# Fused attention block, 8 rows a group: row constant and shift by plain tensor additions, x transposes moved on the TensorE queue

## The chip, the cores and the metric

One core of a Trainium2 chip runs the whole kernel. The metric is the device time of the launch in microseconds; lower is better. Before the change the median of 3 runs is 5887.01 us (5886.72 to 5887.08).

## What is computed

The input `x` has shape (64, 128, 128, 64) in float32: 8192 independent rows of 128 tokens with 64 channels. With all names cut down, the reference is

```python
xn = (x - mean) * rsqrt(var + 0.001) * gamma + beta
q, k, v = xn @ Wq + bq, xn @ Wk + bk, xn @ Wv + bv
scores = einsum('bhid,bhjd->bhij', q, k) * 64 ** -0.5
out = softmax(scores, -1) @ v
return xn + out @ Wo + bo
```

## The kernel before, in words

**Folding.** The normalization and the weights are folded once at the start. Per row of tokens the kernel then needs `g = w_g^T x + g_bias`, scores `g^T x`, softmax, `u = x^T P^T` and `o = u^T w_o`. The output is `y = attn + x_scaled_rows`, where `attn` is `o` times the inverted sum of the softmax and `x_scaled_rows` is the residual with all output biases.

**Shift of the softmax.** The exponential takes a negative shift as its bias. The row constant is the dot product of `x` with a weight row (`row_const`, a reduction over 64 channels of the second half of `x_weighted`) plus a scalar `const_bias`. `top` is that plus the row maximum of the scores (`row_max`); `neg_top` is that minus `top`. Each of these is 128x8 (8 rows of a group).

**Tiling.** A group is 8 rows (`GROUP`), 1024 groups in all. All engines work through the same software pipeline: `pipeline` calls `step(r, t, peeled)` for each t; inside the loop body 8 steps are unrolled, and every engine's queue is the order written by hand in its own `step`. Tiles have 2, 4 or 8 buffers, with rings of semaphores counting their uses.

**Order on each engine in step t** (the number is the group):

- GpSimd (POOL): `x_weighted`(t+2), line 231, 128x1024, after `const_found`(t); `x_scaled_rows`(t+2), line 236; `y`(t-3), line 245, after `attn`(t-3). All three are tensor_tensor instructions with both inputs in SBUF.
- VectorE (DVE): reciprocal `inv_sum`(t-3), line 365; `attn`(t-3), line 370; `row_max`(t), line 376, after the scores; copy `uT`(t-2), line 385; `top`(t), line 392; `neg_top`(t), line 395; `row_const`(t+1), line 401, after `x_weighted`(t+1); copy `xT`(t+2), line 409, after the x transposes.
- TensorE (PE): scores(t), line 456; `u`(t-2) into `ux_ps`, line 467, after `xT`(t+1) is copied out of that bank; first half of the probability transposes (t-1), line 443; `g`(t+1), line 483; second half of them (t-1), line 443 too; x transposes (t+2) into `ux_ps`, line 498, after `uT`(t-2) is copied out; `o`(t-2), line 508.
- ScalarE (ACT): copy of the first transposed half (t-1), line 264; `g`(t+1), line 271; copy of the second half (t-1), line 277; eight exponentials (t), line 287, after `neg_top`(t).
- SyncE (SP): load of group t+4, store of group t-3.

`attn` reads `o_ps` (PSUM) and `inv_sum` (SBUF); `row_max`, `uT` and `xT` read PSUM alone; the `row_const` reduction reads one SBUF tensor; `top` and `neg_top` read two SBUF tensors and one pointer scalar from SBUF.

Of the kernel before, what the change touches and what calls it, by code (L numbers as in the profile page):

```python
# [11 lines left out]
GROUP = 8  # L12
# [5 lines left out]
def build(nc: bass.Bass, x, gamma, beta, mean, var, wq, bq, wk, bk, wv, bv, wo, bo, out):  # L18
# [10 lines left out]
    with ExitStack() as ctx:  # L29
        def sb(name, shape, dtype=F32):  # L30
            return ctx.enter_context(nc.sbuf_tensor(name, shape, dtype))
# [7 lines left out]
        def sem_ring(name, size=SEMS):  # L39
            return [sem(f"{name}{i}") for i in range(size)]  # L40
# [4 lines left out]
        g = sb("g", [128, 4, PAIRS, W])  # L45
        x_weighted = sb("x_weighted", [128, 2, GROUP, 2, C])
        x_scaled_rows = sb("x_scaled_rows", [128, 8, GROUP, C])
        row_const = sb("row_const", [128, 4, GROUP])
        row_max = sb("row_max", [128, 4, GROUP])
        top = sb("top", [128, 4, GROUP])  # L50
# [49 lines left out]
        max_found = sem_ring("max_found")  # L100
        top_found = sem_ring("top_found")
        neg_top_found = sem_ring("neg_top_found")
        const_found = sem_ring("const_found")
        probs_a_found = sem_ring("probs_a_found")
        probs_b_found = sem_ring("probs_b_found")
# [104 lines left out]
        @block.gpsimd  # L210
        def _(pool):
            nc.gpsimd.memset(ident[:], 0.0).then_inc(pool_const, 1)
            nc.gpsimd.memset(w_g[:], 0.0).then_inc(pool_const, 1)
            nc.gpsimd.memset(w_o[:], 0.0).then_inc(pool_const, 1)
            pool.wait_ge(pool_const, POOL_CONSTS)
            nc.gpsimd.affine_select(out=ident[:], in_=ident[:], compare_op=ALU.not_equal, fill=1.0, base=0,
                                    pattern=[[-1, 128]], channel_multiplier=1).then_inc(pool_const, 1)

            weights_b = row_weights[:, None, :, :].broadcast_to([128, GROUP, 2, C])
            bias_b = out_bias[:, None, :].broadcast_to([128, GROUP, C])  # L220
            pool.wait_ge(dve_setup, DVE_READY)

            def step(r, t, peeled):
                n = t + 2
                if exists(r, n, peeled):
                    s = parts(n)
                    pool.wait_ge(x_loaded[n % 8], load_uses(r, n))
                    if exists(r, n - 2, peeled):
                        pool.wait_ge(const_found[parts(n - 2)], uses(r, n - 2))
                        pool.wait_ge(x_scaled[parts(n - 2)], uses(r, n - 2))  # L230
                    nc.gpsimd.tensor_tensor(x_weighted[:, n % 2], x_in[:, n % 8, :, None, :].broadcast_to([128, GROUP, 2, C]),  # L231
                                            weights_b, ALU.mult).then_inc(x_weighed[s], 1)
                    pool.wait_ge(x_weighed[s], uses(r, n))
                    if exists(r, n - 8, peeled):
                        pool.wait_ge(y_found[s], uses(r, n - 8))
                    nc.gpsimd.tensor_tensor(x_scaled_rows[:, n % 8], x_weighted[:, n % 2, :, 0, :], bias_b,  # L236
                                            ALU.add).then_inc(x_scaled[s], 1)
                n = t - 3
                if exists(r, n, peeled):
                    s = parts(n)  # L240
                    pool.wait_ge(attn_kept[s], uses(r, n))
                    pool.wait_ge(x_scaled[s], uses(r, n))
                    if exists(r, n - 4, peeled):
                        pool.wait_ge(y_stored[s], dma_uses(r, n - 4))
                    nc.gpsimd.tensor_tensor(y[:, s], attn[:, s], x_scaled_rows[:, n % 8], ALU.add).then_inc(y_found[s], 1)  # L245

            pipeline(pool, step, dma=True)
# [49 lines left out]
        def _(dve):  # L297
# [62 lines left out]
            def step(r, t, peeled):  # L360
                n = t - 3
                if exists(r, n, peeled):
                    s = parts(n)
                    dve.wait_ge(probs_b_found[s], uses(r, n))
                    nc.vector.reciprocal(inv_sum[:, s, :], prob_sum[:, s, :]).then_inc(sum_inverted[s], 1)  # L365
                    dve.wait_ge(sum_inverted[s], uses(r, n))
                    dve.wait_ge(o_made[s], uses(r, n))
                    if exists(r, n - 4, peeled):
                        dve.wait_ge(y_found[s], uses(r, n - 4))  # L369
                    nc.vector.tensor_tensor(attn[:, s], o_rows, inv_sum[:, s, :, None].broadcast_to([128, GROUP, C]),  # L370
                                            ALU.mult).then_inc(attn_kept[s], 1)
                n = t
                if exists(r, n, peeled):
                    s = parts(n)
                    dve.wait_ge(scores_made[s], uses(r, n))
                    nc.vector.tensor_reduce(row_max[:, s, :].rearrange("p (k h) -> p h k", h=2),  # L376
                                            score_ps[n % 2][:].rearrange("p h (k w) -> p h k w", k=PAIRS),
                                            AX_X, ALU.max).then_inc(max_found[s], 1)
                n = t - 2
                if exists(r, n, peeled):  # L380
                    s = parts(n)
                    dve.wait_ge(u_made[s], uses(r, n))
                    if exists(r, n - 2, peeled):
                        dve.wait_ge(o_made[parts(n - 2)], uses(r, n - 2))
                    nc.vector.tensor_copy(uT[:, n % 2], ux_ps[:].rearrange("p (k w) -> p k w", k=PAIRS)) \  # L385
                        .then_inc(u_kept[s], 1)
                n = t
                if exists(r, n, peeled):
                    s = parts(n)
                    dve.wait_ge(max_found[s], uses(r, n))  # L390
                    dve.wait_ge(const_found[s], uses(r, n))
                    nc.vector.scalar_tensor_tensor(top[:, s, :], row_const[:, s, :], const_bias[:, 0:1], row_max[:, s, :],  # L392
                                                   ALU.add, ALU.add).then_inc(top_found[s], 1)
                    dve.wait_ge(top_found[s], uses(r, n))
                    nc.vector.scalar_tensor_tensor(neg_top[:, s, :], row_const[:, s, :], const_bias[:, 0:1], top[:, s, :],  # L395
                                                   ALU.add, ALU.subtract).then_inc(neg_top_found[s], 1)
                n = t + 1
                if exists(r, n, peeled):
                    s = parts(n)
                    dve.wait_ge(x_weighed[s], uses(r, n))  # L400
                    nc.vector.tensor_reduce(row_const[:, s, :], x_weighted[:, n % 2, :, 1, :],  # L401
                                            AX_X, ALU.add).then_inc(const_found[s], 1)
                n = t + 2
                if exists(r, n, peeled):
                    s = parts(n)
                    dve.wait_ge(xT_made[s], uses(r, n))
                    if exists(r, n - 4, peeled):
                        dve.wait_ge(scores_made[s], uses(r, n - 4))
                    nc.vector.tensor_copy(xT[:, s], ux_ps[:].rearrange("p (k w) -> p k w", k=PAIRS)) \  # L409
                        .then_inc(xT_kept[s], 1)  # L410

            pipeline(dve, step)

        @block.tensor
        def _(pe):
# [30 lines left out]
            def step(r, t, peeled):  # L446
# [31 lines left out]
                if exists(r, n, peeled):  # L478
                    s = parts(n)
                    pe.wait_ge(xT_kept[s], uses(r, n))  # L480
                    if exists(r, n - 1, peeled):
                        pe.wait_ge(g_kept[parts(n - 1)], uses(r, n - 1))
                    nc.tensor.matmul(g_ps[:], w_g_all, xT[:, s].rearrange("p k w -> p (k w)"),  # L483
                                     start=True, stop=True).then_inc(g_made[s], 1)
                n = t - 1
                if exists(r, n, peeled):
                    s = parts(n)
                    pe.wait_ge(probs_b_found[s], uses(r, n))
                    pe.wait_ge(probsT_a_kept[s], uses(r, n))
                    transposed_probs(n, HALF).then_inc(probsT_b_made[s], 1)  # L490
                n = t + 2
                if exists(r, n, peeled):
                    s = parts(n)
                    pe.wait_ge(x_loaded[n % 8], load_uses(r, n))
                    if exists(r, n - 4, peeled):
                        pe.wait_ge(u_kept[parts(n - 4)], uses(r, n - 4))
                    for k in range(PAIRS):
                        last = nc.tensor.transpose(ux_ps[:, k * W:(k + 1) * W],  # L498
                                                   x_in[:, n % 8, 2 * k:2 * k + 2, :].rearrange("p s c -> p (s c)"), ident[:])
                    last.then_inc(xT_made[s], 1)  # L500
                n = t - 2
                if exists(r, n, peeled):
                    s = parts(n)
# [29 lines left out]
```

## Time and profile before

| what | value |
|---|---|
| median of 3 runs | 5887.01 us |
| the profiled execution | 5891.6 us |
| its span (first to last instruction) | 5889.8 us |
| PE busy | 5650.5 us (96%) |
| DVE busy | 5769.4 us (98%) |
| ACT busy | 4783.0 us (81%) |
| POOL busy | 4992.3 us (85%) |
| granted TensorE clock, mean | 0.999 |
| HBM traffic over the span | 91 GB/s |

The profiled execution is 4.6 us above the median. Busy time of an engine counts from an instruction's start to its end as recorded, and it includes time in which an instruction that has started stands still. A steady step of the pipeline works on one group on each engine, so the span is near 1024 times the length of a step plus the filling and draining. In a timeline, the time between the starts of neighbouring instructions on one engine says more than their durations, since neighbouring instructions can overlap by some tens of nanoseconds.

### The profile page before, as it was taken

Reading aid. Unit: us, or ns where it says so; the run is one execution under the profiler, and the core shown is the slowest. Engines: PE = TensorE matmul, PEld = TensorE weight load, DVE = VectorE, ACT = ScalarE, POOL = GpSimd, SP = SyncE. Lnnn points to the kernel's source line nnn. Section 1 sums busy time; section 2 is a strip of 40 time slices with the busy share of each in tenths; the row PEclk is TensorE's granted clock in tenths of the full one; section 3 lists DMA queues with packets and bytes.
Section 4 is the critical chain, followed back from the end, with each engine's and each line's share of the span. In section 5 each row is a group of like instructions: output and inputs, shape, how many; then the busy total and the mean of one; then the engine's idle time right before and its main releaser. Section 6 shows DMA issues by size and latency. Waiting matters only on the chain.

```text
span 5889.8 us, 169868 instructions
## 1 busy us (share of the span) xinstructions
PE 5650.5 (96%) x55320; PEld 4441.6 (75%) x55320; DVE 5769.4 (98%) x8226; ACT 4783.0 (81%) x19460; POOL 4992.3 (85%) x3080
## 2 busy tenths in 40 slices
PE   7999999999999999999999999999999999999999
PEld 6777777777777777777777777777777777777777
DVE  8999999999999999999999999999999999999999
ACT  6888888888888888888888888888888888888887
POOL 7888888888888888888888888888888888888887
PEclk9999999999999999999999999999999999999999
DMA  3444444444444444444444444444444444444443
GB/s 76 91 93 93 92 91 91 93 93 91 91 92 93 93 91 91 93 93 92 91 91 93 93 91 91 92 93 93 91 91 92 93 92 91 91 93 93 91 91 85
DMA packets 2131546, 537.56 MB, mean 91 GB/s; under 512 B 2131520, under 2 KB 2131520, under 8 KB 2131520
## 3 DMA queue, kind: packets, MB, share of 16 engines
q1 hardware_dynamic: 2131520, 537.23, 41.6%
q8 instruction: 14, 0.23, 0.0%
q14 instruction: 12, 0.10, 0.0%
HBM read 268.67 MB, written 268.44 MB: 91 GB/s over the span
## 4 chain that ended last, share of the span: by engine, by line
PE 68%; DVE 23%; issue 8%; DVEq 1%; POOL 0%; SPq 0%; ACT 0%; DMA 0%; POOLq 0%
PE probsT_ps L443 17%; PE ux_ps L467 17%; PE o_ps L508 14%; PE g_ps L483 13%; DVE xT L409 11%; DVE row_const L401 8%; PE ux_ps L498 7%; DVE top L392 2%; DVE uT L385 1%; DVE row_max L376 1%; DVEq L369 1%; DVEq L156 0%; DVE inv_sum L365 0%; PE score_ps L456 0%; POOL y L245 0%
## 5 line engine op out<-in xcount | busy, mean ns | idle before, releaser
L287 ACT ACTIVATE probs<-score_ps,neg_top 128x128 f32<-128x128 f32 x8192 | 2874.9, 376 | 686.1 <-DVE neg_top L395 686.1
L231 POOL TENSOR_TENSOR x_weighted<-x_in,row_weights 128x1024 f32<-128x1024 f32 x1024 | 2427.1, 2370 | 789.1 <-issue 675.9
L287 ACT ACTIVATION_READ_ACCUMULATOR probs<-score_ps,neg_top 128x1 f32 x8192 | 1765.5, 216 | 0.0
L443 PEld LDWEIGHTS probsT_ps<-ident,probs 128*128 128x128 f32 x8192 | 859.0, 140 | 915.0 <-issue 727.4
L236 POOL TENSOR_TENSOR x_scaled_rows<-x_weighted,out_bias 128x512 f32<-128x512 f32 x1024 | 1307.4, 1277 | 90.8 <-POOL x_weighted L231 20.2
L443 PE MATMUL probsT_ps<-ident,probs 128*128 128x128 f32 x8192 | 1315.5, 283 | 5.9 <-ACT probs L287 3.7
L467 PE MATMUL ux_ps<-probsT,x_in 128*64 128x128 f32 x16384 | 1120.8, 278 | 203.1 <-DVE xT L409 176.7
L245 POOL TENSOR_TENSOR y<-attn,x_scaled_rows 128x512 f32<-128x512 f32 x1024 | 1301.6, 1271 | 13.8 <-DVE attn L370 13.8
L395 DVE SCALAR_TENSOR_TENSOR neg_top<-row_const,const_bias,top 128x8 f32<-128x8 f32 x1024 | 1217.1, 1189 | 36.3
L376 DVE TENSOR_REDUCE row_max<-score_ps 128x8 f32<-128x1024 f32 x1024 | 1243.4, 1214 | 2.2 <-PE score_ps L456 2.0
L456 PE MATMUL score_ps<-xT,g 64*128 64x128 f32 x16384 | 1190.0, 285 | 0.3 <-ACT g L271 0.3
L467 PEld LDWEIGHTS ux_ps<-probsT,x_in 128*64 128x64 f32 x16384 | 895.9, 136 | 376.2 <-issue 300.9
L456 PEld LDWEIGHTS score_ps<-xT,g 64*128 64x128 f32 x16384 | 993.9, 187 | 124.2 <-ACT g L271 1.1
L508 PE MATMUL o_ps<-w_o,uT 128*128 128x128 f32 x8192 | 1082.1, 275 | 0.8 <-DVE uT L385 0.8
L483 PE MATMUL g_ps<-xT,w_g 128*128 128x512 f32 x2048 | 1050.3, 595 | 0.9 <-DVE xT L409 0.9
L508 PEld LDWEIGHTS o_ps<-w_o,uT 128*128 128x128 f32 x8192 | 995.3, 192 | 1.0 <-DVE uT L385 1.0
L271 ACT ACTIVATE g<-g_ps,g_bias 128x512 f32<-128x512 f32 x1024 | 703.8, 687 | 290.4 <-PE g_ps L483 290.3
L392 DVE SCALAR_TENSOR_TENSOR top<-row_const,const_bias,row_max 128x8 f32<-128x8 f32 x1024 | 816.6, 798 | 0.1
L370 DVE TENSOR_TENSOR attn<-o_ps,inv_sum 128x512 f32<-128x512 f32 x1024 | 707.9, 691 | 53.0 <-issue 5.7
L264 ACT ACTIVATE probsT<-probsT_ps 128x512 f32<-128x512 f32 x1024 | 611.5, 597 | 107.3 <-PE probsT_ps L443 3.0
L385 DVE COPY uT<-ux_ps 128x512 f32<-128x512 f32 x1024 | 696.8, 680 | 0.6 <-PE ux_ps L467 0.6
L409 DVE COPY xT<-ux_ps 128x512 f32<-128x512 f32 x1024 | 690.8, 675 | 3.8 <-PE ux_ps L498 3.8
(66 smaller groups left out, 2908.1 us busy)
## 6 DMA issues: line engine op xcount, KB each, us to landing
x_in<-in_x SPq DMA_DIRECT2D x1024, 256.0 KB, 3.2
out<-y SPq DMA_DIRECT2D x1024, 256.0 KB, 2.8
norm_row<-in_L_conv_gamma SPq DMA_DIRECT2D x1, 32.0 KB, 3.7
norm_row<-in_L_conv_beta SPq DMA_DIRECT2D x1, 32.0 KB, 3.7
norm_row<-in_L_conv_moving_mean SPq DMA_DIRECT2D x1, 32.0 KB, 4.2
norm_row<-in_L_conv_moving_var SPq DMA_DIRECT2D x1, 32.0 KB, 4.3
norm_row<-in_L_conv_bo SPq DMA_DIRECT2D x1, 32.0 KB, 4.5
w_raw<-in_L_conv_Wq SPq DMA_DIRECT2D x1, 16.0 KB, 1.9
```

Of the source, the lines that this page charges most:

```text
L231: nc.gpsimd.tensor_tensor(x_weighted[:, n % 2], x_in[:, n % 8, :, None, :].broadcast_to([128, GROUP, 2, C]), weights_b, ALU.mult).then_inc ...
L236: nc.gpsimd.tensor_tensor(x_scaled_rows[:, n % 8], x_weighted[:, n % 2, :, 0, :], bias_b, ALU.add).then_inc(x_scaled[s], 1)
L245: nc.gpsimd.tensor_tensor(y[:, s], attn[:, s], x_scaled_rows[:, n % 8], ALU.add).then_inc(y_found[s], 1)
L287: last = nc.scalar.activation(probs[:, n % 2, q, :], score_ps[n % 2][:, q % 2, q // 2 * W:(q // 2 + 1) * W], ACT.Exp, bias=neg_top[:, s, q ...
L376: nc.vector.tensor_reduce(row_max[:, s, :].rearrange("p (k h) -> p h k", h=2), score_ps[n % 2][:].rearrange("p h (k w) -> p h k w", k=PAIR ...
L395: nc.vector.scalar_tensor_tensor(neg_top[:, s, :], row_const[:, s, :], const_bias[:, 0:1], top[:, s, :], ALU.add, ALU.subtract).then_inc(n ...
L409: nc.vector.tensor_copy(xT[:, s], ux_ps[:].rearrange("p (k w) -> p k w", k=PAIRS)) \
L443: last = nc.tensor.transpose(probsT_ps[:, (q - first) * W:(q - first + 1) * W], probs[:, n % 2, q, :], ident[:])
L456: last = nc.tensor.matmul(score_ps[n % 2][:, h, k * W:(k + 1) * W], g[half, s, k, :], xT[half, s, k, :], start=True, stop=True)
L467: last = nc.tensor.matmul(ux_ps[h * C:(h + 1) * C, k * W:(k + 1) * W], x_in[:, n % 8, 2 * k + h, :], probsT[:, n % 2, 2 * k + h, :], start ...
L483: nc.tensor.matmul(g_ps[:], w_g_all, xT[:, s].rearrange("p k w -> p (k w)"), start=True, stop=True).then_inc(g_made[s], 1)
L508: last = nc.tensor.matmul(o_ps[:, k * 2 * C:(k + 1) * 2 * C], uT[:, n % 2, k, :], w_o_all, start=True, stop=True)
```

## The change

`row_const` is now made in two instructions: the reduction writes `row_part`, and a tensor_tensor addition of `const_bias`, broadcast over the 8 rows, writes `row_const` at the end of the DVE step, behind the `xT` copy. `top` and `neg_top` become tensor_tensor instructions without a pointer scalar. POOL's wait for the free `x_weighted` buffer is now on `part_found`. On PE the x transposes (t+2) come ahead of the second half of the probability transposes (t-1).

```diff
+        row_part = sb("row_part", [128, 4, GROUP])
...
+        part_found = sem_ring("part_found")
...
                     if exists(r, n - 2, peeled):
-                        pool.wait_ge(const_found[parts(n - 2)], uses(r, n - 2))
+                        pool.wait_ge(part_found[parts(n - 2)], uses(r, n - 2))
                         pool.wait_ge(x_scaled[parts(n - 2)], uses(r, n - 2))
...
                     dve.wait_ge(max_found[s], uses(r, n))
                     dve.wait_ge(const_found[s], uses(r, n))
-                    nc.vector.scalar_tensor_tensor(top[:, s, :], row_const[:, s, :], const_bias[:, 0:1], row_max[:, s, :],
-                                                   ALU.add, ALU.add).then_inc(top_found[s], 1)
+                    nc.vector.tensor_tensor(top[:, s, :], row_const[:, s, :], row_max[:, s, :],
+                                            ALU.add).then_inc(top_found[s], 1)
                     dve.wait_ge(top_found[s], uses(r, n))
-                    nc.vector.scalar_tensor_tensor(neg_top[:, s, :], row_const[:, s, :], const_bias[:, 0:1], top[:, s, :],
-                                                   ALU.add, ALU.subtract).then_inc(neg_top_found[s], 1)
+                    nc.vector.tensor_tensor(neg_top[:, s, :], row_const[:, s, :], top[:, s, :],
+                                            ALU.subtract).then_inc(neg_top_found[s], 1)
                 n = t + 1
                 if exists(r, n, peeled):
                     s = parts(n)
                     dve.wait_ge(x_weighed[s], uses(r, n))
-                    nc.vector.tensor_reduce(row_const[:, s, :], x_weighted[:, n % 2, :, 1, :],
-                                            AX_X, ALU.add).then_inc(const_found[s], 1)
+                    nc.vector.tensor_reduce(row_part[:, s, :], x_weighted[:, n % 2, :, 1, :],
+                                            AX_X, ALU.add).then_inc(part_found[s], 1)
                 n = t + 2
...
                     nc.vector.tensor_copy(xT[:, s], ux_ps[:].rearrange("p (k w) -> p k w", k=PAIRS)) \
                         .then_inc(xT_kept[s], 1)
+                n = t + 1
+                if exists(r, n, peeled):
+                    s = parts(n)
+                    dve.wait_ge(part_found[s], uses(r, n))
+                    nc.vector.tensor_tensor(row_const[:, s, :], row_part[:, s, :], const_bias[:, 0:1].broadcast_to([128, GROUP]),
+                                            ALU.add).then_inc(const_found[s], 1)
...
                     nc.tensor.matmul(g_ps[:], w_g_all, xT[:, s].rearrange("p k w -> p (k w)"),
                                      start=True, stop=True).then_inc(g_made[s], 1)
-                n = t - 1
-                if exists(r, n, peeled):
-                    s = parts(n)
-                    pe.wait_ge(probs_b_found[s], uses(r, n))
-                    pe.wait_ge(probsT_a_kept[s], uses(r, n))
-                    transposed_probs(n, HALF).then_inc(probsT_b_made[s], 1)
                 n = t + 2
...
                     last.then_inc(xT_made[s], 1)
+                n = t - 1
+                if exists(r, n, peeled):
+                    s = parts(n)
+                    pe.wait_ge(probs_b_found[s], uses(r, n))
+                    pe.wait_ge(probsT_a_kept[s], uses(r, n))
+                    transposed_probs(n, HALF).then_inc(probsT_b_made[s], 1)
```

## Rows read from the trace of the kernel before

**Rows 1.** The page: span, and busy time by engine
```profile
span 5889.8 us, 169868 instructions
PE 5650.5 (96%) x55320; PEld 4441.6 (75%) x55320; DVE 5769.4 (98%) x8226; ACT 4783.0 (81%) x19460; POOL 4992.3 (85%) x3080
```

**Rows 2.** Timeline of DVE, one steady step: start us, us, instruction, [idle before]
```profile
5860.85 0.67 DVE L401 TENSOR_REDUCE row_const<-x_weighted 128x8 f32<-128x512 f32 x1
5861.44 0.67 DVE L409 COPY xT<-ux_ps 128x512 f32<-128x512 f32 x1
5862.04 0.18 DVE L365 RECIPROCAL inv_sum<-prob_sum 128x8 f32<-128x8 f32 x1
5862.26 0.69 DVE L370 TENSOR_TENSOR attn<-o_ps,inv_sum 128x512 f32<-128x512 f32 x1
5862.87 1.21 DVE L376 TENSOR_REDUCE row_max<-score_ps 128x8 f32<-128x1024 f32 x1
5864.00 0.68 DVE L385 COPY uT<-ux_ps 128x512 f32<-128x512 f32 x1
5864.60 0.81 DVE L392 SCALAR_TENSOR_TENSOR top<-row_const,const_bias,row_max 128x8 f32<-128x8 f32 x1
5865.44 1.19 DVE L395 SCALAR_TENSOR_TENSOR neg_top<-row_const,const_bias,top 128x8 f32<-128x8 f32 x1
5866.55 0.67 DVE L401 TENSOR_REDUCE row_const<-x_weighted 128x8 f32<-128x512 f32 x1
```

**Rows 3.** Timelines at the end of the kernel: DVE, then the next POOL instruction
```profile
5870.30 0.22 DVE L392 SCALAR_TENSOR_TENSOR top<-row_const,const_bias,row_max 128x8 f32<-128x8 f32 x1
5870.56 0.23 DVE L395 SCALAR_TENSOR_TENSOR neg_top<-row_const,const_bias,top 128x8 f32<-128x8 f32 x1
5870.70 0.68 DVE L401 TENSOR_REDUCE row_const<-x_weighted 128x8 f32<-128x512 f32 x1
...
5872.81 1.27 POOL L245 TENSOR_TENSOR y<-attn,x_scaled_rows 128x512 f32<-128x512 f32 x1 [2.81 <-DVE attn L370]
```

**Rows 4.** Timeline of POOL in the step of rows 2
```profile
5861.65 2.37 POOL L231 TENSOR_TENSOR x_weighted<-x_in,row_weights 128x1024 f32<-128x1024 f32 x1 [0.75 <-issue]
5864.10 1.29 POOL L236 TENSOR_TENSOR x_scaled_rows<-x_weighted,out_bias 128x512 f32<-128x512 f32 x1
5865.33 1.28 POOL L245 TENSOR_TENSOR y<-attn,x_scaled_rows 128x512 f32<-128x512 f32 x1
```

**Rows 5.** Timelines at the start of the kernel: DVE and POOL
```profile
34.82 2.25 DVE L392 SCALAR_TENSOR_TENSOR top<-row_const,const_bias,row_max 128x8 f32<-128x8 f32 x1
...
34.70 2.35 POOL L231 TENSOR_TENSOR x_weighted<-x_in,row_weights 128x1024 f32<-128x1024 f32 x1
```

**Rows 6.** Instruction groups of DVE: busy us, mean ns | idle before
```profile
L395 DVE SCALAR_TENSOR_TENSOR neg_top<-row_const,const_bias,top 128x8 f32<-128x8 f32 x1024 | 1217.1, 1189 | 36.3
L392 DVE SCALAR_TENSOR_TENSOR top<-row_const,const_bias,row_max 128x8 f32<-128x8 f32 x1024 | 816.6, 798 | 0.1
...
L328 DVE TENSOR_TENSOR b_row<-row_weights,norm_row 128x64 f32<-128x64 f32 x1 | 0.2, 224 | 0.0
...
L322 DVE TENSOR_TENSOR ab_col<-col_tmp,norm_col 64x1 f32<-64x1 f32 x1 | 0.2, 152 | 0.0
```

**Rows 7.** Timeline of PE, one steady step
```profile
5856.56 1.09 PE L467 MATMUL ux_ps<-probsT,x_in 128*64 128x128 f32 x16 [0.21 <-DVE xT L409]
...
5859.02 0.63 PE L443 MATMUL probsT_ps<-ident,probs 128*128 128x128 f32 x4
5859.48 0.60 PE L498 MATMUL ux_ps<-ident,x_in 128*128 128x128 f32 x4
5859.92 1.06 PE L508 MATMUL o_ps<-w_o,uT 128*128 128x128 f32 x8
...
5862.26 1.09 PE L467 MATMUL ux_ps<-probsT,x_in 128*64 128x128 f32 x16 [0.19 <-DVE xT L409]
```

**Rows 8.** Timeline of ACT: the first exponential of the same step
```profile
5860.96 0.37 ACT L287 ACTIVATE probs<-score_ps,neg_top 128x128 f32<-128x128 f32 x1 [0.65 <-DVE neg_top L395]
```

## The prediction

> **What bounds the kernel now.** I read the busy shares first: DVE 98%, PE 96%, ACT 81%, POOL 85% of the span [rows 1]. DVE looks like the bound, and PE close behind. The timeline says what DVE's 98% is made of. One step lasts 5866.55 - 5860.85 = 5.70 us, and two instructions on only 8 elements per partition take 0.84 and 1.11 us of it, counted from start to start [rows 2]. They are not working in that time. At the end of the kernel, while POOL stands idle (its next instruction shows 2.81 us of idle before it, back to 5870.00), the same two take 0.22 and 0.23 us [rows 3].
>
> What they wait for shows in POOL's timeline of the same step [rows 4]. `x_scaled_rows` ends at 5864.10 + 1.29 = 5865.39 and `top` at 5864.60 + 0.81 = 5865.41. `y` ends at 5865.33 + 1.28 = 5866.61 and `neg_top` at 5865.44 + 1.19 = 5866.63. Each ends 0.02 us behind the POOL instruction that was running when it was issued. At the start of the kernel `top` stood for 2.25 us, to 37.07, while POOL's `x_weighted` ran to 37.05 [rows 5]. The means of 798 and 1189 ns over 1024 groups say that this is so all the way [rows 6]. I call this "held": the DVE instruction stands until POOL's is over.
>
> This closes a loop between the two engines. From the start of `row_const`, POOL starts `x_weighted` 0.80 us later, `x_scaled_rows` 2.45 later, `y` 1.23 later, `y` lasts 1.28, `neg_top` is held until its end, and the next `row_const` starts 0.06 before that end: 0.80 + 2.45 + 1.23 + 1.28 - 0.06 = 5.70 us [rows 2, 4]. That is the step. PE fits in: its step is 5.70 with 0.19 us of waiting for `xT`, so 5.51 of its own [rows 7].
>
> **Which instructions are held.** Unheld in the midst of POOL's work run `attn`, a TENSOR_TENSOR with one input in PSUM and one in SBUF (0.69 us, wholly inside `x_weighted`), `inv_sum` with one SBUF input, `row_max` and the copies from PSUM [rows 2, 4]. Three things set `top` and `neg_top` apart: their kind, the pointer scalar, and two tensors that both lie in SBUF. The change takes away the first two and keeps the third. No row shows a plain addition of two SBUF tensors beside a running POOL instruction, so this has to be chosen. A pointer is one value per partition, read once; a second tensor is a stream of its own, and POOL's instructions are streams from SBUF as well. `attn` shows that the plain kind with one such stream goes free, which leaves the second stream as the likeliest cause. I take it: `top` and `neg_top` can still be held, and the new `row_const` addition (`row_part` and the broadcast `const_bias`, both in SBUF) can be held too.
>
> The Trainium skill, page "SBUF — State Buffer", section "Who interferes with whom", says the same: a DVE instruction with two SBUF inputs contends with a GpSimd instruction that reads SBUF, one with at most one such input does not, and the later of the two blocks for the whole of the other. The 2.25 us above agrees with blocking for the whole instruction; by that rule the sum would be the one below.
>
> **The change, part by part.** All times are from the start of the reduction (`row_part`), steps from [rows 2, 4].
>
> *The wait moved to `part_found`*: the same reduction signals, so POOL starts `x_weighted` at 0.80 as before, and ends it at 0.80 + 2.37 = 3.17. Cost nothing.
>
> *The added addition*: the reduction takes 0.59 to the next start, `xT` 0.60, so the addition is issued at 1.19, with `row_part` ready since 0.67. `x_weighted` has been running since 0.80: the addition is held from 1.19 to 3.17 + 0.02 = 3.19. Queued behind it in order are `inv_sum`, `attn`, `row_max`, `uT`, `top`, `neg_top`: everything of the next step. The next starts 0.08 before its end (as the reduction does behind `neg_top` [rows 2]), at 3.11 where it stood at 1.19. DVE loses 1.92 us here.
>
> *The holds that this buys back*: `inv_sum` 3.11, `attn` 3.33 (to 4.02), `row_max` 3.94, `uT` 5.07, `top` issued at 5.67. POOL runs `x_scaled_rows` from 3.25 and `y` from 4.48 (`attn` is ready at 4.02) to 5.76. So `top` is held for at most 0.09 us and `neg_top` not at all, as POOL's next `x_weighted` needs the next reduction. Unheld, the plain additions take: 0.152 us with one element, 0.224 with 64 [rows 6], so about 0.16 with 8. `top` ends at 5.67 + 0.16 = 5.83 (which covers the hold), `neg_top` starts 0.04 later (as in [rows 3]), ends at 6.03, and the reduction starts 0.09 before that [rows 3]: **5.94 us** a step. The bounds: the scalar forms' own times (0.26 and 0.14 from start to start [rows 3]) give 5.67 + 0.40 = 6.07; if the plain additions cost less than 0.16 the end of `y` sets 5.76 + 0.02 + 0.04 + 0.16 - 0.09 = 5.89 at least. I take 5.94, since the nearest rows by kind are the plain additions.
>
> *The x transposes moved ahead*: they need `uT`, which now ends at 5.07 + 0.68 = 5.75. PE then waits for it: the transposes run from about 5.80, the second probability half 0.44 later (6.24), `o` 0.46 after that (6.70), scores and `u`(t-1) start 2.34 - 0.19 = 2.15 after `o` (8.85) [rows 7], end at 9.94, and DVE copies `uT` at 5.07 + 5.94 = 11.01: 1.07 to spare. `xT` needs the transposes at 5.80 + 0.60 = 6.40 and is issued at 5.94 + 0.59 = 6.53: 0.13 to spare. In the old order the transposes would stand behind the second half, which can start 2.46 after `u` [rows 7], at 8.85 - 5.94 + 2.46 = 5.37 or when its copy is through, and would be ready at about 6.43: 0.10 to spare. The move is worth nothing here, at most 0.05 us a step either way. The exponentials cannot start before 5860.96 - 0.65 - 5859.02 = 1.29 us after the second half's start [rows 7, 8], at 7.53 instead of with `neg_top` at 6.03. Who waits for them: ACT is busy 4783.0 / 1024 = 4.67 us a step [rows 1], so 1.27 of a 5.94 us step is free, and the first probability half of the next step is asked for only at 9.94. Nothing.
>
> *Sum*: 5.94 - 5.70 = 0.24 us a step. Over 1024 groups, less a few of filling and draining (some 1015), 244 us. The profiled execution took 5891.6 us; 5891.6 + 244 = 6135.6. It lies 4.6 above the median, so I forecast **6131 us**. The bounds 5.89 and 6.07 give +193 and +376: 6080 to 6263.
>
> **The rivals.**
>
> *Plain additions are not held (faster).* The holds end with the scalar forms. DVE then has 5.70 - 0.84 - 1.11 = 3.75 us of other work and about 0.40 for three additions: 4.15. POOL has 4.96 from the start of `x_weighted` to the end of `y` [rows 4] and no longer waits for DVE's held instruction. PE becomes the bound at 5.51 us: -0.19 a step, -193, **5694 us**. For it: `attn` is of this kind and goes free. Against it: `attn` has one SBUF input.
>
> *Only the two shifts are held, the added one is not (no change).* A broadcast column might not count as a second stream. Then the addition costs 0.08 at 1.19, `top` is issued at 3.75 and held to the end of `x_scaled_rows` at 4.54, `neg_top` to the end of `y`, and the loop of 5.70 stands: **5887 us**. Also the same if the compiler's form were the old one. Nothing in the rows speaks for it but that no broadcast addition is in them.
>
> *All held, and the late `uT` costs more (slower still).* With 0.13 us to spare in front of `xT`, a late `uT` or a wait at the loop's turn shifts PE's transposes behind DVE. Each 0.1 us would add 100 us; with the 6.07 bound and 0.05 of this it would be **6310 us**.
>
> **How the numbers follow.** Held, 5.89 to 6.07 with its own small terms: 0.82. Held with PE's wait on top: 0.04. Not held: 0.09. No change: 0.05. A measurement of this kernel can tell about 0.2%, 12 us, from no change. So slower 0.86, same 0.05, faster 0.09. The range takes the bounds of the held case and some of the third rival: 6075 to 6290; it leaves out the other signs (0.14) and some of the tails.
>
> **What would show it.** If right: the profile of the changed kernel shows the line of the added addition with a mean near 2.0 us, ending 0.02 us behind `x_weighted`; `top` and `neg_top` near 0.16 to 0.2 us; POOL idle about 1.0 us ahead of `x_weighted` (0.80 of it from the reduction); DVE still near 98% busy; PE down to about 93% with its waiting now in front of the x transposes, for `uT`. Wrong at the root: an addition of 0.16 us inside `x_weighted`, DVE near 75% and PE near 99% busy. Wrong in size: `top` held in full by `y`, which would mean that DVE comes round earlier than 5.67, or DVE idle in front of `xT`.

## The result, and the profile after

The changed kernel takes 6140.03 us, median of 4 runs (6139.69 to 6140.2), against 5886.86 us before on the same chip: ratio 1.0431, 95% interval 1.0418 to 1.0443. It is slower by 253 us; 6131 was forecast, in a range of 6075 to 6290. The profiled execution has a span of 6138.2 us.

The page of the changed kernel: its span, its busy times and the costliest group of DVE (busy us, mean ns | idle before):

```profile
span 6138.2 us, 170892 instructions
PE 5661.7 (92%) x55320; PEld 4419.0 (72%) x55320; DVE 6019.2 (98%) x9250; ACT 4793.1 (78%) x19460; POOL 4975.6 (81%) x3080
L417 DVE TENSOR_TENSOR row_const<-row_part,const_bias 128x8 f32<-128x8 f32 x1024 | 1996.6, 1950 | 0.0
```

Two more groups of DVE:

```profile
L397 DVE TENSOR_TENSOR neg_top<-row_const,top 128x8 f32<-128x8 f32 x1024 | 170.7, 167 | 35.4
L394 DVE TENSOR_TENSOR top<-row_const,row_max 128x8 f32<-128x8 f32 x1024 | 161.9, 158 | 0.1
```

The shares of busy time look almost as before [rows 1], and DVE still shows 98%. What fills it is another thing. `top` and `neg_top` fell from 798 and 1189 ns [rows 6] to 158 and 167. The added addition of 8 elements takes 1950 ns on average.

One steady step on DVE (start us, us), as [rows 2]:

```profile
2999.42 0.68 DVE L403 TENSOR_REDUCE row_part<-x_weighted 128x8 f32<-128x512 f32 x1
3000.04 0.69 DVE L411 COPY xT<-ux_ps 128x512 f32<-128x512 f32 x1
3000.65 1.97 DVE L417 TENSOR_TENSOR row_const<-row_part,const_bias 128x8 f32<-128x8 f32 x1
3002.53 0.19 DVE L367 RECIPROCAL inv_sum<-prob_sum 128x8 f32<-128x8 f32 x1
3002.76 0.69 DVE L372 TENSOR_TENSOR attn<-o_ps,inv_sum 128x512 f32<-128x512 f32 x1
3003.37 1.21 DVE L378 TENSOR_REDUCE row_max<-score_ps 128x8 f32<-128x1024 f32 x1
3004.50 0.68 DVE L387 COPY uT<-ux_ps 128x512 f32<-128x512 f32 x1
3005.10 0.15 DVE L394 TENSOR_TENSOR top<-row_const,row_max 128x8 f32<-128x8 f32 x1
3005.29 0.17 DVE L397 TENSOR_TENSOR neg_top<-row_const,top 128x8 f32<-128x8 f32 x1
3005.37 0.68 DVE L403 TENSOR_REDUCE row_part<-x_weighted 128x8 f32<-128x512 f32 x1
```

The same step on POOL, as [rows 4]:

```profile
3000.23 2.36 POOL L233 TENSOR_TENSOR x_weighted<-x_in,row_weights 128x1024 f32<-128x1024 f32 x1 [1.01 <-issue]
3002.67 1.28 POOL L238 TENSOR_TENSOR x_scaled_rows<-x_weighted,out_bias 128x512 f32<-128x512 f32 x1
3003.90 1.27 POOL L247 TENSOR_TENSOR y<-attn,x_scaled_rows 128x512 f32<-128x512 f32 x1
```

The step is 3005.37 - 2999.42 = 5.95 us. The addition is issued 0.42 us after `x_weighted` has started and ends at 3002.62, 0.03 behind it (3002.59). POOL is through with `y` at 3005.17, 0.07 us into `top`, which takes 0.15 us all the same (to 3005.25); `neg_top` meets no POOL instruction. So neither shift is lengthened. Before, the DVE step paid 0.84 and 1.11 us for the shifts. Now it pays 0.19 and 0.08 for them and 1.88 for the addition: 0.20 us more, and 0.05 more for the other instructions together. That is the 5.95 in the place of 5.70.

On PE the waiting has moved in front of the x transposes:

```profile
3003.87 1.02 PE L491 MATMUL g_ps<-xT,w_g 128*128 128x512 f32 x2
3005.33 0.63 PE L500 MATMUL ux_ps<-ident,x_in 128*128 128x128 f32 x4 [0.43 <-DVE uT L387]
3005.79 0.60 PE L451 MATMUL probsT_ps<-ident,probs 128*128 128x128 f32 x4
```

### The profile page after: what moved, and what is told of

The parts are those of the page before. It is cut to its first block, busy times and chain, and to the rows that moved or that the text cites. A ratio compares the mean times of both kernels' runs of the same rounds, so it can differ in the third digit from the quotient of the medians.

```text
span 6138.2 us, 170892 instructions
## 1 busy us (share of the span) xinstructions
PE 5661.7 (92%) x55320; PEld 4419.0 (72%) x55320; DVE 6019.2 (98%) x9250; ACT 4793.1 (78%) x19460; POOL 4975.6 (81%) x3080
## 4 chain that ended last, share of the span: by engine, by line
DVE 38%; issue 31%; PE 29%; DVEq 1%; POOL 0%; SPq 0%; DMA 0%; ACT 0%; POOLq 0%
DVE row_const L417 19%; PE o_ps L516 13%; DVE uT L387 11%; PE ux_ps L500 9%; PE probsT_ps L451 6%; DVE row_max L378 3%; DVE inv_sum L367 2%; DVE row_part L403 1%; DVE attn L372 1%; DVEq L371 1%; DVE xT L411 0%; DVEq L158 0%; DVE top L394 0%; POOL y L247 0%; DVE neg_top L397 0%
## 5 line engine op out<-in xcount | busy, mean ns | idle before, releaser
L417 DVE TENSOR_TENSOR row_const<-row_part,const_bias 128x8 f32<-128x8 f32 x1024 | 1996.6, 1950 | 0.0
L289 ACT ACTIVATION_READ_ACCUMULATOR probs<-score_ps,neg_top 128x1 f32 x8192 | 1856.9, 227 | 0.0
L500 PEld LDWEIGHTS ux_ps<-ident,x_in 128*128 128x128 f32 x4096 | 429.2, 140 | 1261.0 <-issue 1258.8
L247 POOL TENSOR_TENSOR y<-attn,x_scaled_rows 128x512 f32<-128x512 f32 x1024 | 1299.7, 1269 | 15.6 <-DVE attn L372 15.6
L451 PE MATMUL probsT_ps<-ident,probs 128*128 128x128 f32 x8192 | 1286.8, 280 | 4.0 <-ACT probsT L266 2.1
L279 ACT ACTIVATE probsT<-probsT_ps 128x512 f32<-128x512 f32 x1024 | 612.1, 598 | 826.5 <-PE probsT_ps L451 826.5
L500 PE MATMUL ux_ps<-ident,x_in 128*128 128x128 f32 x4096 | 643.3, 280 | 444.6 <-DVE uT L387 442.5
L451 PEld LDWEIGHTS probsT_ps<-ident,probs 128*128 128x128 f32 x8192 | 907.7, 140 | 181.1 <-issue 176.1
L475 PEld LDWEIGHTS ux_ps<-probsT,x_in 128*64 128x64 f32 x16384 | 873.3, 136 | 124.1
L266 ACT ACTIVATE probsT<-probsT_ps 128x512 f32<-128x512 f32 x1024 | 611.5, 597 | 207.1 <-PE probsT_ps L451 207.1
```

The costliest lines, as they stand in the source:

```text
L289: last = nc.scalar.activation(probs[:, n % 2, q, :], score_ps[n % 2][:, q % 2, q // 2 * W:(q // 2 + 1) * W], ACT.Exp, bias=neg_top[:, s, q ...
L417: nc.vector.tensor_tensor(row_const[:, s, :], row_part[:, s, :], const_bias[:, 0:1].broadcast_to([128, GROUP]), ALU.add).then_inc(const_fo ...
L451: last = nc.tensor.transpose(probsT_ps[:, (q - first) * W:(q - first + 1) * W], probs[:, n % 2, q, :], ident[:])
L475: last = nc.tensor.matmul(ux_ps[h * C:(h + 1) * C, k * W:(k + 1) * W], x_in[:, n % 8, 2 * k + h, :], probsT[:, n % 2, 2 * k + h, :], start ...
L500: last = nc.tensor.transpose(ux_ps[:, k * W:(k + 1) * W], x_in[:, n % 8, 2 * k:2 * k + 2, :].rearrange("p s c -> p (s c)"), ident[:])
```

## The experiments

The theory: DVE instructions that need what POOL's instructions use stand until the running POOL instruction ends. The change swaps two short holds for one of nearly the whole of `x_weighted`. Rivals: the scalar form is what gets held; the move on PE costs; one more instruction in the queue costs.

The diffs below are shortened: indices, waits and semaphores are left out, and where only the order changes it is written in words. Each is against the changed kernel, unless the kernel before or another one is named. Each ratio is against the kernel before on the same chip.

### The old order on TensorE

```diff
-    x transposes (t+2), second probability half (t-1)
+    second probability half (t-1), x transposes (t+2)
```

> The changed kernel with the old order on TensorE (second half of the probability transposes ahead of the x transposes). Theory (DVE's queue, with the added addition held by x_weighted, is the loop): the x transposes start when uT is copied in either order, and the second half fits in the idle time in front of them, so the step stays 5.95 us and the time 6140, within 15 us. Rival (the moved transposes carry part of the loss): the time falls by 0.05 to 0.2 us a step, to 5940 to 6090.

Measured: 6143.7 us, ratio 1.0434 (1.0417 to 1.0452) against 1.0431 with the move. PE (in the kernel with the old order) waits at the same place, for the same copy:

```profile
3000.67 0.63 PE L451 MATMUL probsT_ps<-ident,probs 128*128 128x128 f32 x4
3001.61 0.63 PE L506 MATMUL ux_ps<-ident,x_in 128*128 128x128 f32 x4 [0.32 <-DVE uT L387]
```

The move carries none of the loss.

### Only the two shifts as plain additions

```diff
 (the kernel before)
-nc.vector.scalar_tensor_tensor(top, row_const, const_bias, row_max, ALU.add, ALU.add)
+nc.vector.tensor_tensor(top, row_const, row_max, ALU.add)
-nc.vector.scalar_tensor_tensor(neg_top, row_const, const_bias, top, ALU.add, ALU.subtract)
+nc.vector.tensor_tensor(neg_top, row_const, top, ALU.subtract)
```

> The kernel before with top and neg_top as plain additions and nothing added or moved; const_bias is left out of the shift. Theory (a second tensor from SBUF is what gets held, whatever the kind of instruction): both are still held to the ends of x_scaled_rows and y, the loop of 5.70 us stands, 5887 us within 12. Rival (the scalar form is what is held): both take 0.16 us, DVE falls to near 75% busy, PE bounds at 5.51 us, about 5694 us.

Measured: 5886.3 us, ratio 0.9997 (0.9987 to 1.0007). The groups of DVE in this kernel:

```profile
L395 DVE TENSOR_TENSOR neg_top<-row_const,top 128x8 f32<-128x8 f32 x1024 | 1215.6, 1187 | 35.2
L392 DVE TENSOR_TENSOR top<-row_const,row_max 128x8 f32<-128x8 f32 x1024 | 814.9, 796 | 0.1
```

796 and 1187 ns, where the scalar forms had 798 and 1189 [rows 6]. For these two, the scalar form and its pointer make no difference. This settles the choice that the forecast had to make.

### The added instruction with one SBUF input

```diff
-nc.vector.tensor_tensor(row_const, row_part, const_bias.broadcast, ALU.add)
+nc.vector.tensor_reduce(row_const, row_part[:, s, :, None], AX_X, ALU.add)
```

> The changed kernel with the added addition replaced by a reduction over one element, which has one SBUF input and copies row_part; const_bias is left out. Theory: it goes unheld inside x_weighted (about 0.1 us), so top and neg_top come round early again and are held by x_scaled_rows and y: step 5.70, 5887 us within 15. Rival (the extra step in DVE's queue or the move on TensorE costs, not the second input): the time stays above 6000 us.

Measured: 5877.44 us, ratio 0.9981 (0.9971 to 0.9991). The groups of DVE:

```profile
L417 DVE TENSOR_REDUCE row_const<-row_part 128x8 f32<-128x8 f32 x1024 | 147.6, 144 | 0.0
L397 DVE TENSOR_TENSOR neg_top<-row_const,top 128x8 f32<-128x8 f32 x1024 | 1218.2, 1190 | 35.1
L394 DVE TENSOR_TENSOR top<-row_const,row_max 128x8 f32<-128x8 f32 x1024 | 725.9, 709 | 0.1
```

One place in its timeline, DVE and then POOL:

```profile
3007.77 0.14 DVE L417 TENSOR_REDUCE row_const<-row_part 128x8 f32<-128x8 f32 x1
3007.84 0.18 DVE L367 RECIPROCAL inv_sum<-prob_sum 128x8 f32<-128x8 f32 x1
...
3007.38 2.36 POOL L233 TENSOR_TENSOR x_weighted<-x_in,row_weights 128x1024 f32<-128x1024 f32 x1 [0.75 <-issue]
```

At the same place in the queue and with `x_weighted` running, an instruction of the same size is through in 144 ns, and the holds on the shifts are back. `top` takes 0.09 us less than before (709 against 798 ns), near the 0.07 us by which the added instruction puts off the next one: a held instruction absorbs what is put ahead of it.

### The addition ahead of the xT copy

```diff
     reduction -> row_part
+    addition -> row_const
     copy -> xT
-    addition -> row_const
```

> The changed kernel with the addition straight behind the reduction, ahead of the xT copy. Theory (held only if a POOL instruction has already started): it is issued about 0.72 us after the reduction's start, just ahead of x_weighted at 0.80, takes 0.16 us and can push x_weighted back to 0.90 at most; top and neg_top are held again; step 5.70 to 5.80, 5887 to 5990 us. Rival (x_weighted gets in first): held to 3.19 with xT behind it, step 6.54, about 6740 us.

Measured: 5877.4 us, ratio 0.9982 (0.9972 to 0.9991), with all the arithmetic of the changed kernel. That is 10 us below the range that was expected, which took the kernel before for the least. A step of it, DVE and then POOL:

```profile
3003.55 0.67 DVE L403 TENSOR_REDUCE row_part<-x_weighted 128x8 f32<-128x512 f32 x1
3004.26 0.17 DVE L409 TENSOR_TENSOR row_const<-row_part,const_bias 128x8 f32<-128x8 f32 x1
...
3004.36 2.36 POOL L233 TENSOR_TENSOR x_weighted<-x_in,row_weights 128x1024 f32<-128x1024 f32 x1 [0.75 <-issue]
```

The addition starts 0.10 us ahead of `x_weighted` and takes 0.17 us. POOL still starts 0.81 us after the reduction and takes its 2.36 us. So one and the same instruction takes 1.95 us or 0.17 us by its place in DVE's queue: it starts 1.23 us behind the reduction's start or 0.71.

### The addition as tensor_scalar, with a pointer and with an immediate

```diff
-nc.vector.tensor_tensor(row_const, row_part, const_bias.broadcast, ALU.add)
+nc.vector.tensor_scalar(row_const, row_part, const_bias[:, 0:1], None, ALU.add)
```

> The changed kernel with the added addition as a tensor_scalar: one SBUF tensor and a pointer scalar; the result is the same number. Theory (only a second SBUF tensor is held): unheld as the one-input reduction was, 5877 us within 10. Rival (the Trainium skill, page SBUF - State Buffer, section Who interferes with whom: a tensor_scalar from SBUF to SBUF can run in a mode that takes both ports, and then it contends with GpSimd too): held by x_weighted like the addition, about 1.95 us, 6140 us. A third reading, that a pointer scalar alone is held, gives 6140 as well.

Measured: 6138.23 us, ratio 1.042 (1.0402 to 1.0437). My theory, that only a second tensor is held, fell here. One SBUF tensor and a pointer are held as well. A pointer or the form could be why, so the pointer went:

```diff
 (the kernel with the pointer)
-nc.vector.tensor_scalar(row_const, row_part, const_bias[:, 0:1], None, ALU.add)
+nc.vector.tensor_scalar(row_const, row_part, 0.25, None, ALU.add)
```

> The changed kernel with the added addition as a tensor_scalar with an immediate of 0.25 in the place of the pointer to const_bias: one SBUF tensor, no pointer scalar (the constant is another one). If the form from SBUF to SBUF is what is held: about 1.95 us, 6138 us. If the pointer scalar was what was held in the run with it: unheld, 5877 us.

Measured: 6136.57 us, ratio 1.0423 (1.0405 to 1.044). The first group of DVE in each kernel, the pointer's first, then the immediate's:

```profile
L417 DVE TENSOR_SCALAR row_const<-row_part,const_bias 128x8 f32<-128x8 f32 x1024 | 2006.3, 1959 | 0.0
```

```profile
L417 DVE TENSOR_SCALAR row_const<-row_part 128x8 f32<-128x8 f32 x1024 | 1999.5, 1953 | 0.0
```

That a tensor_scalar is slow by itself is ruled out by the end of the same traces, where POOL has no more `x_weighted` to do. In the kernel with the immediate, DVE and then POOL's next instruction, idle since 6112.72:

```profile
6114.44 0.17 DVE L417 TENSOR_SCALAR row_const<-row_part 128x8 f32<-128x8 f32 x1
...
6116.45 1.27 POOL L247 TENSOR_TENSOR y<-attn,x_scaled_rows 128x512 f32<-128x512 f32 x1 [3.73 <-DVE attn L372]
```

There it takes 0.17 us, and 0.23 us with the pointer. So a tensor_scalar from SBUF to SBUF is held, without any pointer too, and what is held is wider than the forecast had it. It is as the Trainium skill has it on the page "SBUF — State Buffer", section "Who interferes with whom": copies and tensor_scalar can run in a mode with both ports and then contend with GpSimd too, while a reduction does not, as the 144 ns above agree. The same section frees an instruction with at most one SBUF input only outside such modes. Which mode VectorE ran in shows in no trace here.

### Only the move on TensorE

```diff
 (the kernel before)
-    second probability half (t-1), x transposes (t+2)
+    x transposes (t+2), second probability half (t-1)
```

> The kernel before with only the x transposes moved ahead of the second half of the probability transposes. Theory: the loop POOL - neg_top - row_const of 5.70 us does not touch PE, and uT is ready 0.05 to 0.13 us before the transposes' new place: 5887 us within 10. Rival (PE waits for uT and hands it on): up to 0.1 us a step, 5990 us.

Measured: 5888.96 us, ratio 0.9997 (0.9987 to 1.0007). No difference, as was expected where PE is not the bound.

### No held instruction on VectorE: two ways

The first way keeps all of the arithmetic and moves it. ScalarE adds the constant behind its exponentials; GpSimd makes the shifts behind `y`:

```diff
+nc.scalar.activation(row_const, row_part, ACT.Identity, bias=const_bias)
+nc.gpsimd.tensor_tensor(top, row_const, row_max, ALU.add)
+nc.gpsimd.tensor_tensor(neg_top, row_const, top, ALU.subtract)
-nc.vector.tensor_tensor(row_const, row_part, const_bias.broadcast, ALU.add)
-nc.vector.tensor_tensor(top, row_const, row_max, ALU.add)
-nc.vector.tensor_tensor(neg_top, row_const, top, ALU.subtract)
```

> The whole of the change's arithmetic with no addition of two SBUF tensors left on VectorE: ScalarE adds the constant to row_part, GpSimd makes top and neg_top behind y. Theory (the holds alone keep the step at 5.70): VectorE needs 3.75 us, GpSimd 4.91 plus two small additions of some 0.2 us with their waits, TensorE bounds at 5.51 us: 5694 us, up to 5800 if the two small additions push GpSimd over 5.51. Rival (something else than the holds keeps 5.70, such as TensorE's waits for copies): 5870 us or more.

Measured: 5582.18 us, ratio 0.9477 (0.9461 to 0.9493). POOL in this kernel:

```profile
2998.72 2.37 POOL L233 TENSOR_TENSOR x_weighted<-x_in,row_weights 128x1024 f32<-128x1024 f32 x1
3001.17 1.27 POOL L238 TENSOR_TENSOR x_scaled_rows<-x_weighted,out_bias 128x512 f32<-128x512 f32 x1
3002.39 1.28 POOL L247 TENSOR_TENSOR y<-attn,x_scaled_rows 128x512 f32<-128x512 f32 x1
3003.63 0.21 POOL L253 TENSOR_TENSOR top<-row_const,row_max 128x8 f32<-128x8 f32 x1
3003.92 0.20 POOL L256 TENSOR_TENSOR neg_top<-row_const,top 128x8 f32<-128x8 f32 x1
3004.10 2.35 POOL L233 TENSOR_TENSOR x_weighted<-x_in,row_weights 128x1024 f32<-128x1024 f32 x1
...
3015.20 2.35 POOL L233 TENSOR_TENSOR x_weighted<-x_in,row_weights 128x1024 f32<-128x1024 f32 x1 [0.38 <-issue]
...
3041.99 2.36 POOL L233 TENSOR_TENSOR x_weighted<-x_in,row_weights 128x1024 f32<-128x1024 f32 x1
```

On GpSimd the two shifts cost 0.47 us (3003.63 to 3004.10), where VectorE had stood 1.95 us for them. They now stand in one queue with what had held them. GpSimd has no slack left for it, though: eight steps take 3041.99 - 2998.72 = 43.27 us, 5.41 each, and one of the eight, from 3009.43 to 3015.20, takes 5.77 us with 0.38 us of idle time that no other engine's work ends. The whole is faster than both kernels: 308 us below the 5890.46 of the one before on the same chip. It lies 112 us below the 5694 that was expected, since TensorE's own step is shorter than was taken, and shorter again in the moved order (both below).

The second way leaves the shifts out; the negated maximum is the shift, and the row constant (which cancels in the softmax) is still reduced but used for nothing:

```diff
 (the kernel before)
-nc.vector.tensor_reduce(row_max, scores, AX_X, ALU.max)
+nc.vector.tensor_reduce(neg_top, scores, AX_X, ALU.max, negate=True)
-nc.vector.scalar_tensor_tensor(top, row_const, const_bias, row_max, ALU.add, ALU.add)
-nc.vector.scalar_tensor_tensor(neg_top, row_const, const_bias, top, ALU.add, ALU.subtract)
```

> The kernel before without top and neg_top: the reduction over the scores writes the negated maximum, which is the shift; the row constant is still reduced but goes nowhere (it cancels in the softmax). Theory: no hold is left, VectorE needs 3.75 us a step, TensorE bounds at 5.51: 5694 us, within 25. Rival (TensorE is held up by the latency of the copies): between 5720 and 5887.

Measured: 5615.59 us, ratio 0.9533 (0.9517 to 0.9549). It lies 78 us below the 5694 that was expected, outside the 25 allowed: PE's own step is shorter than I took it for (below).

### The move where TensorE is the bound

The first way above has the moved order, the second has not. Each was run with the other one.

```diff
 (the kernel with the negated maximum)
-    second probability half (t-1), x transposes (t+2)
+    x transposes (t+2), second probability half (t-1)
```

> The kernel with the negated maximum as shift, and the x transposes moved ahead of the second half of the probability transposes. Theory (where TensorE is the bound the move is worth something: its step was 5.44 us in the old order with the negated maximum, and 5.33 us in the new order with the shifts on GpSimd): 0.11 us a step less, about 5505 us. Rival (the 5.33 us came from the shifts being on GpSimd): 5616 us as without the move.

Measured: 5506.68 us, ratio 0.9352 (0.9337 to 0.9368).

```diff
 (the kernel with the constant on ScalarE and the shifts on GpSimd)
-    x transposes (t+2), second probability half (t-1)
+    second probability half (t-1), x transposes (t+2)
```

> The kernel with the constant on ScalarE and the shifts on GpSimd, with TensorE's old order. Theory (the order is worth 0.11 us where TensorE bounds): 5.44 us a step in the place of 5.33, 5582 + 112 = 5694 us at most, 5616 at least, as GpSimd was nearly as long there. Rival (the order is worth nothing): 5582 us.

Measured: 5617.84 us, ratio 0.9541 (0.9525 to 0.9557). PE, first the negated maximum in the old order, then in the moved order:

```profile
3004.57 1.02 PE L473 MATMUL g_ps<-xT,w_g 128*128 128x512 f32 x2
3005.51 0.63 PE L433 MATMUL probsT_ps<-ident,probs 128*128 128x128 f32 x4
3005.98 0.60 PE L488 MATMUL ux_ps<-ident,x_in 128*128 128x128 f32 x4
3006.42 0.83 PE L498 MATMUL o_ps<-w_o,uT 128*128 128x128 f32 x6
```

```profile
3004.91 1.02 PE L473 MATMUL g_ps<-xT,w_g 128*128 128x512 f32 x2
3005.77 0.60 PE L482 MATMUL ux_ps<-ident,x_in 128*128 128x128 f32 x4
3006.21 0.60 PE L433 MATMUL probsT_ps<-ident,probs 128*128 128x128 f32 x4
3006.64 1.06 PE L498 MATMUL o_ps<-w_o,uT 128*128 128x128 f32 x8
```

From `g` to `o` it is 1.85 us in the old order and 1.73 in the moved one. The weight load in front of the second probability half waits for the copy of the first, in the old order right behind `g` (ACT, and the loads of TensorE):

```profile
3004.77 0.60 ACT L264 ACTIVATE probsT<-probsT_ps 128x512 f32<-128x512 f32 x1 [0.61 <-PE probsT_ps L433]
```

```profile
3005.48 0.42 PEld L433 LDWEIGHTS probsT_ps<-ident,probs 128*128 128x128 f32 x4 [0.72 <-issue]
```

The copy ends at 3005.37 and the load starts 0.11 us later, too late to run beside `g` (which takes 0.86 us from start to start where the next is ready, so to 3005.43). The x transposes have no such wait. That this is the reason is read from these lines and was not tried by itself; that the move takes the time from 5616 to 5507 us with the negated maximum, and from 5618 to 5582 us with GpSimd's shifts, is measured. With the negated maximum the whole step is PE's, 5.44 us in the old order and 5.34 in the moved one. With GpSimd's shifts the queue of GpSimd is 5.41 us a step, which leaves less to gain; that this is the limit there is read from its rows and was not tried by itself.

## Why the prediction was right

- **What bounds before.** The loop `x_weighted`, `x_scaled_rows`, `y`, held `neg_top`, reduction was the bound: with the holds gone, and nothing else changed on PE, the time falls to 5616 us.
- **The choice (a plain addition of two SBUF tensors is held).** Right, by the run with only the shifts changed. The reason given, that a second stream makes the difference, was too narrow: a one-tensor tensor_scalar is held too, a one-tensor reduction not. The forecast's account of the Trainium skill had the same gap, since it left out the modes with both ports. This did not touch the sum, because every addition of the change has two SBUF tensors. The rival "the broadcast column does not count" fell with the first profile. Its working has a slip: with the 0.08 us of the addition `top` is issued at 3.83 and not at 3.75 (3.82 with one SBUF input), still ahead of 4.54, so its 5887 us stands.
- **The terms.** The hold was put from 1.19 to 3.19 and measured from 1.23 to 3.20 after the reduction's start; the plain additions were put at 0.16 and measured at 0.15 and 0.17; `top` was put at 5.67 and came at 5.68; the step 5.94 against 5.95. The error of the whole, 6131 against 6140, is about that 0.01 us over a thousand steps. The 0.04 us by which the addition is issued late cost nothing, as POOL sets its end. The lower bound of 5.89 was not one: it took 0.16 us for an addition that it supposed shorter.
- **PE.** The wait for `uT` was foreseen; it is 0.43 us. The 0.13 us to spare between the x transposes and the `xT` copy measured 0.03 (3005.96 to 3005.99): the transposes start 0.15 us behind the end of `uT` (3005.18 to 3005.33), where 0.05 was put. That this cost nothing was close, and in part luck. The moved order was put at nothing, within 0.05, and is worth nothing there. It was not put in words that it would pay once PE bounds.
- **The faster rival's size.** The 5694 us took PE's own step as 5.70 less the 0.19 us of shown waiting. PE took 5.44 in the old order, and 5.34 in the order of the change, where the run without holds measured 5507 us. Part of its wait for `xT` was hidden: from the scores to `u` it is 1.35 us before [rows 7] (the scores start at 5860.91 in that timeline) and 1.09 when nothing waits, which is 0.26 and not 0.19.
- **What stayed open.** Two kernels with the step back at 5.70 (one SBUF input; addition ahead of `xT`) are 10 us below the one before, 0.01 us a step. Their traces show where: `x_weighted` takes 2359 and 2362 ns on average against 2370, and `x_scaled_rows` 1269 and 1270 against 1277. Why GpSimd is that much quicker there, no run tells. Whether a POOL instruction that reads nothing from SBUF would hold DVE was not tried.

## What to carry to other kernels

When a tiny instruction shows a mean near a microsecond, compare its end with the ends of the other engine's instructions before thinking of its arithmetic. On VectorE, an addition of two SBUF tensors, or a tensor_scalar from SBUF to SBUF, cost what was left of the GpSimd instruction that it met (here always one with two SBUF inputs); put it where GpSimd is idle, give it to GpSimd or ScalarE, or fold it into a reduction. A held instruction hides what is ahead of it, so its removal pays only if no other one comes to stand in a longer GpSimd instruction, and a reordering that pays nothing now can pay once the hold is gone.

## What the runs showed of the hardware

- Held to the end of GpSimd's instruction: tensor_tensor with two SBUF inputs (1950 ns beside `x_weighted`, 0.15 to 0.17 us alone), and tensor_scalar from SBUF to SBUF with a pointer (1959 ns, 0.23 us alone) or an immediate (1953 ns, 0.17 us alone). That the one with the pointer is held was not expected.
- Not held: a reduction from SBUF to SBUF of the same 8 elements (144 ns), and a reciprocal of 8 elements from SBUF to SBUF (186 ns on average before, 0.18 us wholly inside `x_weighted` [rows 2, 4]). So not every elementwise instruction from SBUF to SBUF is held.
- An addition that starts 0.10 us ahead of GpSimd's instruction goes through (168 ns on average) and does not lengthen that one visibly (2.36 us either way).
- GpSimd itself needs 0.20 us for an addition of 8 elements per partition, against 0.15 to 0.17 us on VectorE alone.
